# A two-layer attention and expert kernel: packed constants, another opening, per-expert routing rows, four score banks in the last batch, and products of zeros beside the last maxima of the first batch

## The reference

```
x = x + tanh(g_xattn[0]) * attention0(layernorm(x), ctx, ctx, mask)
x = x + tanh(g_ffn[0])   * experts0(layernorm(x))   # 64 experts, top 8 of 4 groups, cap 128, and a shared one
x = x + tanh(g_xattn[1]) * attention1(layernorm(x), ctx, ctx, energies)
x = x + tanh(g_ffn[1])   * experts1(layernorm(x))   # 8 experts of inner width 352, top 2
attention: softmax(q @ k.T / sqrt(8)) @ v @ Wo + bo ; layer 0 masks the scores,
           layer 1 multiplies the probabilities by sigmoid((mean|energies| - 0.1) * 10)
experts:   sum over experts of w[token, expert] * (silu(x @ gate.T) * (x @ up.T)) @ down
```

## Time and profile before

| | us |
|---|---|
| three runs | 1059.21, 1056.97, 1054.69 (median 1056.97) |
| profiled execution | 1066.47 |
| its span | 1064.7 |
| PE busy | 923.6 (87%) |
| DVE busy | 750.2 (70%) |
| ACT busy | 571.0 (54%) |
| POOL busy | 310.4 (29%) |
| mean granted clock | 0.886 |

### The profile page before, as it was taken

One profiled execution on the slowest core, in us unless ns is written; L12 is line 12 of the kernel. 1 busy time (PEld: TensorE's weight loads), 2 busy tenths in 40 slices (PEclk: granted clock), 3 DMA queues, 4 the chain that ended last, 5 costly groups with the idle time before them and its releaser, 6 DMA issues.

```text
span 1064.7 us, 24592 instructions
## 1 busy us (share of the span) xinstructions
PE 923.6 (87%) x9812; PEld 636.5 (60%) x9812; DVE 750.2 (70%) x1420; ACT 571.0 (54%) x1214; POOL 310.4 (29%) x276
## 2 busy tenths in 40 slices
PE   4469899999999987699997679999999998842996
PEld 3126566666666664588885246666656666532885
DVE  6677677777776718579997966887887782042996
ACT  1315456656566665256663135667666666521664
POOL 2600302112112100157773502143224221002764
PEclk9559899999999998599998658999999997665999
DMA  6670404034032110466550620441343131016652
GB/s 151 115 162 2 110 5 114 30 86 114 29 86 60 28 32 2 128 172 171 166 153 21 158 64 17 98 114 44 72 113 92 24 85 31 2 17 134 166 161 54
DMA packets 49007, 90.01 MB, mean 85 GB/s; under 512 B 21816, under 2 KB 32252, under 8 KB 48892
## 3 DMA queue, kind: packets, MB, share of 16 engines
q1 hardware_dynamic: 48892, 88.44, 34.8%
HBM read 47.32 MB, written 1.75 MB: 46 GB/s over the span
## 4 chain that ended last, share of the span: by engine, by line
PE 63%; DVE 14%; POOL 6%; ACT 6%; DMA 5%; issue 4%; SPq 1%; POOLq 0%; DVEq 0%; ACTq 0%
PE ps L1167 20%; PE po L1188 16%; PE pm L1137 9%; POOL tmpf L771 6%; PE pc L1102 5%; PE ps L1171 4%; PE pc L1115 4%; DVE vaug L533 3%; DVE qsel L524 3%; ACT qsel L941 3%; DMA routing<-vaug 2%; DVE mx_part L420 2%; DVE junk L423 2%; ACT probs L847 1%; DMA wts<-in_experts 1%
## 5 line engine op out<-in xcount | busy, mean ns | idle before, releaser
L847 ACT ACTIVATE probs<-ps 121x400 f32<-121x400 f32 (+1 forms) x768 | 347.7, 502 | 162.1 <-PE ps L1171 92.0
L1167 PE MATMUL ps<-qst,kst 128*121 128x400 f32 (+3 forms) x768 | 301.3, 457 | 15.7 <-ACT probs L847 14.2
L420 DVE TENSOR_REDUCE mx_part<-pm 100x2 f32<-100x964 f32 x192 | 213.6, 1158 | 58.3 <-PE pm L1137 57.6
L1167 PEld LDWEIGHTS ps<-qst,kst 128*121 128x121 f32 (+3 forms) x768 | 140.0, 193 | 108.5 <-ACT probs L847 71.0
L1274 PE MATMUL pm<-qsel,qst 128*128 128x400 f32 x660 | 159.3, 366 | 40.3 <-DVE qsel L524 36.5
L423 DVE CUSTOM_DVE_ANT_0 junk<-pm,negq 100x964 bf16<-100x964 f32 x128 | 143.6, 1159 | 61.8 <-PE pm L1137 61.7
L1188 PE MATMUL po<-probs,vaug 121*32 121x100 f32 x6144 | 182.3, 262 | 1.3 <-ACT probs L847 1.3
L1188 PEld LDWEIGHTS po<-probs,vaug 121*32 121x32 f32 x6144 | 137.7, 114 | 52.6 <-issue 50.1
L1137 PE MATMUL pm<-khi,qbd 32*100 32x482 f32 x768 | 133.9, 488 | 35.8 <-DVE mx_part L420 12.7
L1274 PEld LDWEIGHTS pm<-qsel,qst 128*128 128x128 f32 x660 | 123.5, 197 | 58.8 <-DVE qsel L524 57.7
L771 POOL TENSOR_TENSOR tmpf<-vaug,wb 128x400 f32<-128x400 f32 x55 | 68.5, 1245 | 227.7 <-DMA wb<-routing 166.0
(11 more groups left out here) (179 smaller groups left out, 897.9 us busy)
## 6 DMA issues: line engine op xcount, KB each, us to landing
kst<-khi SPq DMA_DIRECT2D x128, 180.5 KB, 4.0
wb<-routing SPq DMA_DIRECT2D x66, 200.0 KB, 3.8
ctxT<-in_ctxT SPq DMA_DIRECT2D x16, 722.0 KB, 4.3
kst<-klo SPq DMA_DIRECT2D x64, 180.5 KB, 3.9
wts<-in_experts SPq DMA_DIRECT2D x55, 192.0 KB, 3.7
wb<-routing SPq DMA_DIRECT2D x22, 400.0 KB, 4.1
qsel<-qhi SPq DMA_DIRECT2D x16, 100.0 KB, 2.4
kst<-kst SPq DMA_DIRECT2D x7, 180.5 KB, 3.5
```

The lines of the kernel that those rows point to most:

```text
L420: ins = nc.vector.tensor_reduce(parts[:, 2 * i:2 * i + 2, j, x], bank, AX, ALU.max)
L847: nc.scalar.activation(probs[t % 2][0:r, g * GQ:(g + 1) * GQ], ps[0:r, n % 2, 0:GQ], ACT.Exp, scale=SCALE).then_inc(s["probs_ready"], 1)
L1167: mm = nc.tensor.matmul(ps[0:r, n % 2, 0:GQ], kst[b % 2][0:rows, g, t * KEY_TILE:t * KEY_TILE + r], qst[b % 2][0:rows, g * GQ:(g + 1) * GQ ...
```

## The change

- The constants are packed in two tensors (`early`, `late`) and loaded by one DMA each; the small one goes first. The transposed mask is loaded from ACT's queue and has a semaphore of its own.
- PE opens with 16 products of zeros. The first keys come in two parts around the turn of the tokens, the values of batch 0 before ACT's wait for the mask rows. The reduced mask goes to bank `po`, DVE's low parts of the keys stand behind the mask's maximum.
- DVE makes the low part of the queries after the first quad. Gate and bias of the output and the four pieces of the energies move in between later batches.
- SP sends the row of maxima of batch 0 ahead of the stacking of batch 1.
- In the first batch's quads, two products of zeros follow each of the last four, four each of the two ahead.
- The last batch uses four score banks (two of `pm`, which has no maxima left), and all four groups stand ahead of the product with the values.
- Layer 1's weights are written as 8 rows; each read back covers the partitions of one expert's stretch.

```diff
-STRETCHES = [128 // F0, 16]
-SPREADS = [2, 1]
 RING = 4
+def spans_of(l, u):
+    if l == 0:
+        return [(2 * u + i, F0 * i, F0 * i + F0) for i in range(2)]
+    cuts = sorted({128 * u, 128 * u + 128} | {e * I1 for e in range(E1) if 128 * u < e * I1 < 128 * u + 128})
+    return [(lo // I1, lo - 128 * u, hi - 128 * u) for lo, hi in zip(cuts, cuts[1:])]
+def spread_by(l, u):
+    return 16 * sum(len(spans_of(l, v)) for v in range(u % RING, u + 1, RING))
...
+WARM = 16
+IDLE_QUADS, IDLE_EACH, IDLE_LAST = 4, 2, 4
...
+        def score_bank(b, n):
+
+            if b < B - 1:
+                return ps[:, n % 2, :]
+            return (ps[:, 0, :], ps[:, 1, :], pm[:, 2, :], pm[:, 3, :])[n % J]
...
-                dve.wait_ge(mask_in, 48)
+                dve.wait_ge(mask_in, 16)
                 step(nc.vector.tensor_reduce(any_q[:], mask_u[:], AX, ALU.max))
                 several([nc.vector.tensor_scalar(any_two[:, 0:1], any_q[:], BIG, None, ALU.mult),
                          nc.vector.tensor_scalar(any_two[:, 1:2], any_q[:], -BIG, None, ALU.mult),
                          nc.vector.tensor_scalar(any_diag[:], ident[0:S, 0:S], any_q[:, 0:1], None, ALU.mult)], "any_diag")
+                first_k_low(0)
...
-                dve.wait_ge(act_done, ACT_MARK["tanh"])
-                step(nc.vector.tensor_scalar(wo[l][:], wo[l][:], tgates[:, l:l + 1], None, ALU.mult))
-                step(nc.vector.scalar_tensor_tensor(xres[:], bo[l][0:S, :].unsqueeze(1).broadcast_to([S, B, D]),
-                                                    tgates[0:S, l:l + 1], xres[:], ALU.mult, ALU.add))
                 for k in range(QUADS):
                     quad_max(0, k)
+                    if k == 0:
+                        queries_low(l)
                     if k in FIRST_K_TAKEN:
                         k_low(1, FIRST_K_TAKEN.index(k))
                 row_max(0)
                 for k in range(QUADS_AHEAD):
                     quad_max(1, k)
                 slots(0)
+                dve.wait_ge(act_done, ACT_MARK["tanh"])
+                step(nc.vector.tensor_scalar(wo[l][:], wo[l][:], tgates[:, l:l + 1], None, ALU.mult))
+                slots(1)
+                step(nc.vector.scalar_tensor_tensor(xres[:], bo[l][0:S, :].unsqueeze(1).broadcast_to([S, B, D]),
+                                                    tgates[0:S, l:l + 1], xres[:], ALU.mult, ALU.add))
+                slots(2)
+                if l == 0:
+                    energy_sums()
+                slots(3)
+                if l == 0:
+                    energy_scaled()
+                slots(4)
+                if l == 0:
+                    dve.wait_ge(consts_late, 16)
+                    step(nc.vector.tensor_copy(before_b[:], before[:]))
+                slots(5)
                 if l == 0:
                     energy_gates()
-                for b in range(1, B - 1):
-                    slots(b)
+                slots(6)
...
-            first_k(0)
+            act.wait_ge(consts_early, 16)
+            first_k(0, (0,))
             transposed(0)
+            first_k(0, (1, 2))
+            first_v(0)
...
-                    if n >= 2:
+                    if b == B - 1 and t == 0 and g >= 2:
+
+                        pe.wait_ge(s["max_taken"], 2 * QUADS * B)
+                    elif b == B - 1 and t >= 1:
+                        pe.wait_ge(s["probs_ready"], n - 3)
+                    elif n >= 2:
...
+                def idle(count):
+                    for i in range(count):
+                        nc.tensor.matmul(ps[:, i % 2, :], zero_b[:, 0:128], zero_b[:], start=True, stop=True)
...
+                        if b == B - 1:
+                            scores(b, t, 2)
+                            scores(b, t, 3)
+                            weigh(*((b, t - 1) if t >= 1 else (b - 1, KEY_TILES - 1)))
+                            beside(b, t)
+                            continue
...
                     if k in FIRST_K_AFTER:
                         k_chunk(1, FIRST_K_AFTER.index(k))
+                    if k >= QUADS - IDLE_QUADS:
+                        idle(IDLE_EACH)
                 max_rows(0)
                 for k in range(QUADS_AHEAD):
                     max_quad(1, k)
+                    idle(IDLE_LAST)
...
+            for _ in range(WARM):
+                nc.tensor.matmul(ps[:, 0, :], zero_b[:, 0:128], zero_b[:], start=True, stop=True)
+            pe.wait_ge(consts_early, 16)
             pe.wait_ge(pool_init, 3)
-            first_k(0)
+            first_k(0, (0,))
             transpose_tokens(0)
+            first_k(0, (1, 2))
             pe.wait_ge(dve_done, marks["any_diag"])
-
-            pe.wait_ge(A[0]["klo_ready"], 3)
-            step(nc.tensor.matmul(pc[:, 0:S], ones_f[0:S, :], any_diag[:], start=True, stop=True), "any_b")
+            step(nc.tensor.matmul(po[:, 0:S], ones_f[0:S, :], any_diag[:], start=True, stop=True), "any_b")
             queries(0)
+            pe.wait_ge(dve_done, marks["any_b"])
...
                 context(l, 2, 0)
+                row(l, 0)
                 stack(l, 1, 1)
-                row(l, 0)
                 context(l, 3, 1)
...
-                    if l == 0:
-                        for i in range(2):
-                            sp.dma_start(wb[slot][64 * i:64 * i + 64, :],
-                                         scratch[0][bass.ds(u * 2 + i, 1), :].broadcast_to([64, TOK]))\
-                                .then_inc(m["wb_in"][slot], 16)
-                    else:
-                        sp.dma_start(wb[slot][:], scratch[1][bass.ds(u * 16, 16), :].unsqueeze(1)
-                                     .broadcast_to([16, 8, TOK])).then_inc(m["wb_in"][slot], 16)
+                    for row, lo, hi in spans_of(l, u):
+                        sp.dma_start(wb[slot][lo:hi, :], scratch[l][row:row + 1, :].broadcast_to([hi - lo, TOK]))\
+                            .then_inc(m["wb_in"][slot], 16)
...
-                    per = UNITS1 * STRETCHES[1] // E1
-                    sp.dma_start(scratch[1].rearrange("(e s) t -> e s t", s=per),
-                                 wT[0:E1, :].unsqueeze(1).broadcast_to([E1, per, TOK])).then_inc(m["w_out"], 16)
+                    sp.dma_start(scratch[1], wT[0:E1, :]).then_inc(m["w_out"], 16)
```

## The result

| | kernel before | kernel after |
|---|---|---|
| median, us | 1057.05 (4 runs) | 1019.9 (4 runs, 1010.4 to 1023.2) |
| ratio | | 0.963 (95%: 0.956 to 0.971) |
| profiled execution | 1066.47 | 1022.83 |
| its span, mean granted clock | 1064.7, 0.886 | 1021.0, 0.902 |

A forecast was written before the change was run, and what follows sets the result against it. PE was taken as busy nearly all the time in attention, so gains lie only where it waits or runs at half clock. Terms sum to -61.7 on 1066.5, giving 1004.8; less 9.5 for the median, 995, own range 985 to 1006, wider 977 to 1013.

The forecast's parts named there:

- routing write: Before layer 1's experts: writing 8 rows once costs at most 2.8 us in place of 24.1; -21.3, ends -19 and -22.
- opening, up to the first scores, zeros apart: Opening: PE's first maximum at 21.5 in place of 34.65, some costs coming back; -12, ends 0 and -15.
- energies' stall gone in layer 0: Layer 0, batches 1 to 2: excess from PE waiting on DVE's energy sums and a half clock goes; -7.1.
- pieces back between layer 0's batches: Layer 0: bias and energy pieces of DVE, returning between batches, hold PE a little; +2.5, ends 0 and +6.
- bias between layer 1's batches: Layer 1, between batches 1 and 2: DVE's bias overfills a slot; +1.7, ends 0 and +2.2.
- products of zeros, both layers: Beside the last maxima: they raise PE's clock, gaining 2 and 7.8 for 1.6 cost; -8.2, ends +3 and -10.
- bias out of layer 1's maxima, low parts in: In front of layer 1's maxima: the bias leaves and the low parts enter; 0.
- last batch, layer 1: Four score banks make ACT the bound, 30 to 33 us; -13, ends -6 and -16.
- last batch, layer 0, with batch 6: Layer 0's last batch ends with DVE's routing, 36.0 us against 40.3; -4.3, ends 0 and -7.
- The first rival: Clock not raised in layer 1, first or last batch: loses 7.8 and 7, giving 1010; chance 0.22.
- the step to the median: From the profiled execution's forecast, 1004.8, to 995: the median of the runs shown lies 9.5 lower than that execution.
- the two that were named as refuting it: Prediction is wrong if first scores don't come before 70 us, or if the last batches stay over 38 us.

The follow-up runs named there:

- rows128: Changed kernel with layer 1's scores over 128 partitions in place of 97, added query rows zero: 1008.9 us, ratio 0.951.
- keys_early: Changed kernel with batch 2's three key products in slots 1 to 3 of layer 1's first batch, not 4 to 6: 1015.8 us, ratio 0.956.
- zeros_dense: Changed kernel with layer 1's products of zeros in one run of sixteen behind the last maxima ahead: 1011.1 us, ratio 0.954.
- experiment 4: Layer 1's scores over 128 partitions in place of 97: in the changed kernel 1008.9 us, ratio 0.951; alone in the kernel before 1049.4, 0.993.
- routing_only: Kernel before with only the change's routing (eight rows written once, reads per expert's stretch): 1036.2 us, ratio 0.977.
- experiments 1 and 9: Changed kernel without zeros beside maxima, 1013.9 us; three versions adding DVE pieces in slots and 128-row layer 1 scores, 996.8, 995.4, 995.1.
- experiment 8: Steps of the opening and layer 0's end; here the changed kernel without the sixteen opening products of zeros: 1018.6 us, ratio 0.960.

## Why the prediction was wrong

By its own terms, on the profiled execution (forecast, then measured):

| step | forecast | measured |
|---|---|---|
| routing write | -21.3 | -22.4 |
| opening, up to the first scores, zeros apart | -12 | -11.8 |
| energies' stall gone in layer 0 | -7.1 | -7.5 |
| pieces back between layer 0's batches | +2.5 | +8.7 |
| bias between layer 1's batches | +1.7 | +8.4 |
| products of zeros, both layers | -8.2 | +2.1 |
| bias out of layer 1's maxima, low parts in | 0 | -1.1 |
| last batch, layer 1 | -13 | -15.8 |
| last batch, layer 0, with batch 6 | -4.3 | -3.8 |
| sum | -61.7 | -43.2 (whole: -43.7) |

- **The first step that failed** is the price of DVE's pieces: "the two long ones each hold PE by about 1 us and the others by 0.5 in all", and +1.7 in layer 1. It counted DVE's time against DVE's slack and had no term for the clock. The stalls themselves came to 5.7 us in layer 0 (1.7 and 1.4 for the long ones, about 0.6 for each of the four others) and 1.6 to 1.9 in layer 1. So the +1.7 was right, and the +2.5 less than half of its stalls. The falls of the clock under PE's pause came on top: 3 us in layer 0 and 6.5 in layer 1, where it stayed at 0.50 for 16 us. The same trace had shown such a fall already: the energies' 2.12 us had cost 7.1. I had taken the whole 7.1 as gained by moving the step, and then priced its pieces by another rule. That the clock falls was not certain either: in rows128, keys_early and zeros_dense it held in layer 1.
- **The second** is "I take both as gained" for the zeros. The first rival, the clock not raised in layer 1 (1010, chance 0.22), was the case. It lost 7.8 there as it said, and 2 of cost, but not the 7 in the last batch, whose clock stayed up. My argument from layer 0, where the clock rose after two slots, compared layers whose scores differ in height, 128 partitions and 97; in experiment 4 this difference alone moved the rise.
- **The third** is the step to the median. On the profiled execution 18 us are missing, on the median 25. I took 9.5 off because the profile stood that far above the median. But its last batch had a fall of the clock of 8.7 us, and the sum had taken that away once, in the -13 from 45.8. So most of the 9.5 was taken off twice; it makes 6.6 of the 25. routing_only's profile, which has no such fall, plus the 22.4 of the write gives 1032.2 + 22.4 = 1054.6, as fast as the fastest executions of the kernel before (1053.9 to 1054.7). The changed kernel's profile stood only 2.9 above its median, with falls of its own.
- The rule that I set against the rows, that activity releases the clock (the Trainium skill, "TensorE: Matmul & The Clock Gate", "What's actually happening"), would have given +1.6 for the zeros, which is near the +2.1 measured. Its reason there was another one, though: the scores alone did not raise the clock (22 us at 0.50 under a PE counted busy). Read simply, the rule gave the right sum from a wrong picture.
- **The signs.** Neither of the two that were named as refuting it appeared (first scores at 66.0, last batches of 30.3 and 27.7 us). Two of the others failed and pointed at the first two steps: value chunks 41 to 43 us apart throughout, and a clock of 1.00 from the second slot of layer 1.
- **Right for the reasons given:** the routing write, and the reads of one row by 128 partitions, which cost nothing; the row of maxima sent first, without which 5.2 us of the opening would be lost; DVE as the bound of layer 0's last batch.
- **Right by luck:** the last batch of layer 1. It measured -15.8 against a profile that had a fall of 8.7 us in it. Against the other profiles with two banks it is -7 to -8.6. And the sum of the opening: the first maximum came 1.4 us later than forecast, and the 1.3 us that should have come back behind it did not (41.8 us from there to the first scores before and after, zeros apart).

The measured terms are differences of the copies of outputs between the two profiles, with the zeros' share from experiments 1 and 9; in layer 0 it takes 1.2 us as gained by the zeros, which the spread of the other kernels leaves open. What is left to the whole, 0.5 us, lies under the experts' own variation: their first ten units differ by up to 3 us between kernels that have the same ones.

## What to carry to other kernels

Price a stall by what its pause may do to PE's clock and not only by its own length: look in the trace for an earlier stall of that size, and take what that one cost as the upper end. Work of another engine that must go somewhere goes into slots where PE doesn't need that engine next, never at a boundary where it does; here the place counted and not the length of the piece. When a loss seems to have moved with a piece, look at the clock at the piece itself before believing it. If PE is busy and its clock is at half, look at how many partitions its products use before adding products to warm it, and if some are added, add them without a pause. And when a forecast starts from one profile, don't take a fall of its clock off both in a term and in the step to the median.

## What the runs showed of the hardware

- **Height of products and the clock.** Scores over 97 partitions: 0.50 for some 22 us in which PE was counted busy nearly without a break. Over 128, with the same time per product and zeros in the added rows of the queries: 1.00 after 5 us in the changed kernel and 7 in the kernel before (experiment 4).
- **The same pause, with and without a fall.** PE idle for 1.5 of 4 us left its clock at 1.00 in rows128 and keys_early and took it to 0.50 for 16 us in the changed kernel.
- **DVE beside POOL.** The same small steps took several times as long where POOL's product of the queries ran. The cast of `before_b` (100 x 100) took 0.21 us in the kernel before's opening, with POOL idle, and beside that product 1.38 (timeline of the changed kernel):

```profile
110.21 1.39 DVE L533 TENSOR_SCALAR late<-late,tgates 128x128 f32<-128x128 f32 x1
...
284.01 3.29 POOL L747 TENSOR_TENSOR qst<-qsel,late 96x400 fp32r<-96x400 f32 x4 [5.85 <-PE po L1251]
...
284.37 1.38 DVE L546 CAST before_b<-late 100x100 bf16<-100x100 f32 x1
```

The scaling of the output's weights (128 x 128), first row, took 1.39 us behind the start of such a product (at 109.85), 0.28 in layer 1, where it starts 0.2 us ahead of one, and 0.29 in the kernel before's layer 0. The Trainium skill, "Trainium Architecture — The Big Picture", section "What this means for kernel authors", says that VectorE and GpSimd share a port pair with an exclusive lock. The rows agree that they disturb each other; that the lock is the cause no run here isolates.
- **The clock at launch.** The column of the granted clock shows 1.00 in the first microseconds of every kernel, but the products' own times don't agree. Of the sixteen products of zeros at the very start (512 columns each, from 1.67 us on) the first eight start 0.40 to 0.43 us apart, the rest 0.21 to 0.23 (starts in the timeline); in the run of sixteen in layer 1 the same two paces stand where the column says 0.50 and 1.00. And without the sixteen the first two products of the keys take 1.94 us in place of 1.05 (experiment 8), with 1.00 in the column for both. So PE started at half speed, and the column can't be trusted there.
